# Latent attention in a four-layer model: keys mapped per head, scores over 32 rows in row quarters

## The reference, cut to what matters

```python
c_q = h_t @ W_DQ + b_DQ                     # 32 numbers per token
c_kv = h_t @ W_DKV + b_DKV                  # 32
q_c = c_q @ W_UQ + b_UQ;  k_c = c_kv @ W_UK + b_UK     # 128 per head
q_r = c_q @ W_QR + b_QR;  k_r = h_t @ W_KR + b_KR      # 32 per head; k_r is shared
q = concat([q_c, q_r]);   k = concat([k_c, k_r])
attn = softmax(q @ k.T / sqrt(128 + 32))
o = (attn @ (c_kv @ W_UV + b_UV)) @ W_O + b_O
```

## Time and profile before

| | |
|---|---|
| three runs | 4379.04, 4382.91, 4383.27 us, median 4382.91 |
| the profiled execution | span 4374.4 us from its first to its last instruction; of its time outside the span nothing is recorded; the runs' median is 8.5 us longer |
| busy in the span | PE 3697.7 us, DVE 3018.0, ACT 2493.0, POOL 1280.4 |
| the stage `latent_heads` | from about 1094 to 1800 us |

### The profile page before, as it was taken

One profiled execution on the slowest core, in us unless ns is written; L12 is line 12 of the kernel. 1 busy time (PEld: TensorE's weight loads), 2 busy tenths in 40 slices (PEclk: granted clock), 3 DMA queues, 4 the chain that ended last, 5 costly groups with the idle time before them and its releaser, 6 DMA issues. The chain is left out here.

```text
span 4374.4 us, 86127 instructions
## 1 busy us (share of the span) xinstructions
PE 3697.7 (85%) x32769; PEld 1693.5 (39%) x32773; DVE 3018.0 (69%) x4604; ACT 2493.0 (57%) x5084; POOL 1280.4 (29%) x1223
## 2 busy tenths in 40 slices
PE   5769998753999999787999997878995689999957
PEld 4523333633333333342222223445654512222237
DVE  6567774557656665658999994435994489999933
ACT  3436666463244444533888887434543448888844
POOL 2610000524488887000000000035883500000016
PEclk7879999776999999886999999888997879999979
DMA  3221110210000000002000000050001120000012
GB/s 122 71 77 37 41 42 15 82 34 9 1 4 6 4 4 4 17 1 71 25 28 31 28 24 3 18 130 10 1 1 64 56 78 23 31 31 24 19 54 73
DMA packets 80436, 152.55 MB, mean 35 GB/s; under 512 B 20492, under 2 KB 46748, under 8 KB 79132
## 3 DMA queue, kind: packets, MB, share of 16 engines
q1 hardware_dynamic: 54408, 105.15, 7.4%
q0 software_dynamic: 12704, 22.97, 1.8%
q10 hardware_dynamic: 12916, 18.93, 1.3%
HBM read 103.75 MB, written 31.20 MB: 31 GB/s over the span
## 5 line engine op out<-in xcount | busy, mean ns | idle before, releaser
L1516 DVE TENSOR_REDUCE 32_heads_mx<-32_heads_mps 128x1 f32<-128x1024 f32 x512 | 602.4, 1219 | 48.0 <-PE 32_heads_mps L1366 45.5
L1516 DVE TENSOR_REDUCE 55_heads_mx<-55_heads_mps 128x1 f32<-128x1024 f32 x512 | 602.5, 1219 | 46.4 <-PE 55_heads_mps L1366 43.7
L1486 ACT ACTIVATE 32_heads_p<-32_heads_sps 128x512 f32<-128x512 f32 x1024 | 553.7, 596 | 86.4 <-PE 32_heads_sps L1392 83.2
L1486 ACT ACTIVATE 55_heads_p<-55_heads_sps 128x512 f32<-128x512 f32 x1024 | 553.7, 596 | 85.9 <-PE 55_heads_sps L1392 82.6
L2528 ACT ACTIVATE 21_latent_heads_p<-21_latent_heads_ring 128x512 f32<-128x512 f32 x512 | 277.4, 595 | 360.0 <-PE 21_latent_heads_ring L2447 360.0
L1516 DVE TENSOR_REDUCE 7_heads_mx<-7_heads_mps 128x1 f32<-128x1024 f32 (+7 forms) x384 | 333.6, 908 | 147.6 <-PE 7_heads_mps L1374 101.9
L2551 DVE TENSOR_REDUCE 21_latent_heads_mx<-21_latent_heads_ring 128x1 f32<-128x512 f32 x512 | 322.9, 684 | 146.7 <-PE 21_latent_heads_ring L2426 146.7
L1486 ACT ACTIVATE 7_heads_p<-7_heads_sps 128x512 f32<-128x512 f32 (+3 forms) x640 | 308.1, 533 | 156.0 <-PE 7_heads_sps L1395 116.5
L1392 PE MATMUL 32_heads_sps<-30_head_rows_qs,30_head_rows_ks 123*32 123x512 bf16 x4096 | 314.4, 383 | 8.3 <-ACT 32_heads_p L1486 5.0
L1392 PE MATMUL 55_heads_sps<-51_head_rows_qs,51_head_rows_ks 123*32 123x512 bf16 x4096 | 314.3, 383 | 8.2 <-ACT 55_heads_p L1486 5.0
L2443 PE MATMUL 21_latent_heads_ring<-21_latent_heads_qc,17_mla_mem_keys 64*128 64x512 f32 x1024 | 273.0, 610 | 3.6 <-DMA 18_mla_loop_mem_mrow<-21_latent_heads_mT 3.6
...
## 6 DMA issues: line engine op xcount, KB each, us to landing
...
```

Source lines behind the costliest of these rows:

```text
L1486: act.activation(pslot[x % PS][:, 0:CW - off], sps[e % SB][:, 0:CW - off], ACT.Exp, scale=SCALE / 2).then_inc(ex_done, 1)
L1516: dve.tensor_reduce(mx[h % 2][:, i, half:half + 1], mps[x % 2][:, 0:w], AX.X, ALU.max).then_inc(mx_taken, 1)
```

## The change

- Keys go through the head's matrix, not queries. `make_keys` multiplies `maps` (head's matrix, its 32 columns written four times, so that the result stands in all four quarters of the partitions) with `keys`, gives `kh`, 32 rows in each quarter, and ACT copies it out, 1024 columns at a time. `cq` holds c_q alone, in four quarters, for all heads.
- Score and maxima passes contract over 32 rows. Their two matmuls use row quarters 0 and 1 in one pass and 2 and 3 in the next (`rows`).
- What belonged to the row of ones now depends on the key alone: `tilt`, one number for each key and head. It is computed once before head 0 (16 matmuls into `ops`), split in three bfloat16 parts by DVE, turned by 8 transposes, copied by ACT, and carried by 4 DMAs a head into `k_side`, whose other rows are -1. A bfloat16 pair adds it in every maxima pass (with `ones`), and one pair adds it and takes off the maximum in every score pass (`k_side` with `q_side`). The maximum's rows go into `q_side` by 4 DMAs (2 before).
- A ring buffer is now one tensor of 1024 columns; DVE takes one maximum of 1024 columns (32 a head, 64 of 512 before), ACT one exponential of 1024 (64 of 512 before).
- POOL adds up slots 0 to 23 (22 adds a head, two buffers `psum` by turns), DVE slots 24 to 31 into `dsum` (6 adds a head). For head 7 DVE does all. `denominators` moves from slot 4 to slot 6 and goes over both sums, 8 matmuls for 4.
- The product's copy to `osb` moves from DVE to ACT, after slot 1's exponential (DVE for head 7). The copies into `Lh` go. POOL clears `q_side` at the stage's start.
- In `mla_prep` the heads' matrices come ahead of the values on PE; `L` and its copies give way to `maps` and `tilt`, filled by DVE and ACT.

The core of the diff:

```diff
-    SUMS = 4
-    FIRST, LAST = SUMS + 2, 24
+    SUMS = 6
+    FIRST, LAST = 6, 24
+    BY_DVE = tuple(range(24, S))
-        ring = [st.ps(f"ring{i}", [P, CW]) for i in range(2 * RING)]
+        ring = [st.ps(f"ring{i}", [P, 2 * CW]) for i in range(RING)]
...
+        def rows(number, x):
+            low = DC * (2 * (number % 2) + x)
+            return slice(low, low + DC)
...
                 def max_pair(u, h):
-                    i = u // 2
-                    if u % 8 == 0:
-                        pe.wait_ge(q_copied, NC * h + u // 8 + 1)
+                    i, pair = u % NT, u // NT
+                    if i == 0:
+                        pe.wait_ge(k_copied, 2 * h + pair + 1)
...
                     for x in range(2):
-                        half = slice(KC * x, KC * (x + 1))
-                        pe.matmul(bank(number, x)[:], qc[h % 2][half, tile(i)], keys[half, chunk(2 * (u % 2) + x)],
-                                  start=True, stop=True).then_inc(mx_ready, 1)
+                        r = rows(number, x)
+                        pe.matmul(bank(number, x), cq[r, tile(i)], kh[h % 2][r, chunk(2 * pair + x)], start=True, stop=False,
+                                  tile_position=(r.start, 0))
+                    if u == 0:
+                        pe.wait_ge(tilt_in[h % 2], 64 * (h // 2 + 1))
+                    for x in range(2):
+                        r = rows(number, x)
+                        pe.matmul(bank(number, x), ones[r, :], k_side[h % 2][r, chunk(2 * pair + x)], start=False, stop=True,
+                                  tile_position=(r.start, 0)).then_inc(mx_ready, 1)
...
                 def scores(p, h):
...
                     for x in range(2):
-                        half = slice(KC * x, KC * (x + 1))
-                        pe.matmul(bank(number, x)[:], keys[half, tile(j)], qc[h % 2][half, chunk(2 * (p % 2) + x)],
-                                  start=True, stop=False)
+                        r = rows(number, x)
+                        pe.matmul(bank(number, x), kh[h % 2][r, tile(j)], cq[r, chunk(2 * (p % 2) + x)], start=True, stop=False,
+                                  tile_position=(r.start, 0))
...
+                for t in range(NT):
+                    ins = pe.matmul(ops[:, 8 * t:8 * (t + 1)], keys[0:KC, tile(t)], tilt[0:KC, :], start=True, stop=True)
+                ins.then_inc(tilt_ready, 1)
+                pe.wait_ge(tilt_split, 1)
+                for h in range(MLA_H):
+                    ins = pe.transpose(tilt_rows[0:PARTS, h * P:(h + 1) * P], tilt_parts[:, h].rearrange("p a t -> p (a t)"), g.ident_bf[:])
+                ins.then_inc(tilt_turned, 1)
                 for u in range(U):
                     max_pair(u, 0)
...
-                        for x in range(2):
-                            act.wait_ge(sc_ready, 2 * n + x + 1)
...
+                        act.wait_ge(sc_ready, 2 * n + 2)
...
+                        act.activation(slot(p, h)[:], ring[place["score", h, p] % RING][:], ACT.Exp, scale=MLA_SCALE).then_inc(ex_done, 1)
...
+                        if h and p == 1:
+                            act.wait_ge(pv_done, NT * h)
+                            if h >= 2:
+                                act.wait_ge(o_out, 16 * NC * (h - 1))
+                            act.activation(osb[0][:], ops[:], ACT.Identity).then_inc(o_copied, 1)
...
+                            if p in BY_DVE[2:]:
+                                if p == BY_DVE[2] and h:
+                                    dve.wait_ge(z_done, h)
+                                add(dve, dsum, dve_added, DVE_ADDS * h, by_dve[p % 2], by_dve[p % 2].index(p), h)
```

More of the change, by code:

```diff
@@ new lines, in latent_head_loop, with add @@
+        freed = {place["score", h, p]: (ex_done, S * h + p + 1) for h in range(MLA_H) for p in range(S)}
+        freed.update({place["max", h, u]: (mx_taken, U * h + u + 1) for h in range(MLA_H) for u in range(U)})
+        freed.update({place["keys", h, x]: (k_copied, 2 * h + x + 1) for h in range(MLA_H) for x in range(NC // 2)})
+        assert sorted(freed) == list(range(len(passes)))
+        def add(eng, sums, done, base, order, n, h):
+            x = order[n] % 2
+            eng.wait_ge(ex_done, S * h + order[n] + 1)
+            if n > 1:
+                eng.wait_ge(done[x], base + n - 1)
+            so_far = slot(order[0], h)[:] if n == 1 else sums[:, x, :]
+            eng.tensor_tensor(sums[:, x, :], so_far, slot(order[n], h)[:], ALU.add).then_inc(done[x], 1)
@@ L2461, in denominators @@
                 def denominators(h):
-                    pe.wait_ge(added_even, ADDS * (h + 1))
-                    pe.wait_ge(added_odd, ADDS * (h + 1))
+                    last = h == LASTH
+                    for x in range(2):
+                        if not last:
+                            pe.wait_ge(pool_added[x], POOL_ADDS * (h + 1))
+                        pe.wait_ge(dve_added[x], DVE_ADDS * h + (S // 2 - 1 if last else DVE_ADDS))
                     if h:
```

280 lines of the change are left out of this document (148 added, 132 removed).

## The result

The changed kernel took 4387.65 us (median of 17 runs, 4380.95 to 4400.56), the kernel before 4379.18 (17 runs beside it, 4370.60 to 4384.97): a ratio of 1.0022, 95% interval 1.0014 to 1.0031. The medians differ by 8.5 us (0.19%), about the 9 us that I had set as what a measurement tells from no change, and the interval leaves out 1; I had forecast 16 us faster.

The account below looks back on a forecast made before the run. PE bounds the middle piece now (60.60 of 60.60 us); afterwards the buffer ring sets the pace. Terms -21 (heads 1 to 6) - 8 (head 0) + 1 (head 7) + 12 (front) = -16 us: 4367 us, range 4312 to 4425.

Parts of the forecast that it names:

- The price of a pass: PE, score and maxima passes: 1.07 us with no overlap, 0.54 with full overlap of passes in different row quarters.
- Rival (a): PE: matmuls start strictly in written order, so +3.6 us a head and 4419 us in all; chance 0.17.
- Rival (b): PE: one waiting round per quarter, a pass starts 0.43 us behind its neighbour; +3.2 a head, 4389 us; chance 0.20.
- The ring walk: Middle slots: three buffers set the pace, each turning in 2.65 us, 0.88 a pass; six slots take 15.9 us.
- Six slots take 15.9 ... Nineteen: 50.4: Slots 6 to 24: 50.4 us at the six-slot pace; with 6.8 for slots 6 and 7, 57.1 against 60.6.
- Head 0: First head, without denominators: middle piece 50.4 + 1.9 for keys = 52.3 us, a gain of 8.3.
- A longer wait in front puts a few us there, within that bound: Clock at 0.50 around head 0's start: a few us lost, counted inside the front's +12 (8 to 16).
- Before head 0: Latent heads' front: first maximum +11 us, maxima -0.7, two more DMAs +1.5; together +12 (8 to 16).
- The two key passes and their copies lie beside the tilts: Front, before head 0: key passes and copies run alongside the tilts' 4.8 us, with no time of their own.
- Score-only slots: Slots without maxima: -0.05 us per two slots, +0.6 product copy, -0.9 denominators, +0.3 keys; together nothing.
- Rival (c): Middle: VectorE alone bounds it at 44 us, 16.6 less in each of seven heads; 4280 at the full; chance 0.16.
- the stall: Slots 6 and 7: no maximum read during VectorE's 5.2 us of division; 6.8 us more than two steady slots.

Follow-up runs that it names:

- e1_one_pair: The changed kernel with every pass in row quarters 0 and 1; 1.1422 times the kernel before.
- the two profiles of the change: The changed kernel's first run, 1.0022 times the kernel before, and the same kernel run again without an edit, 1.0007.
- e2_busy_pe: The changed kernel with matmuls nobody reads filling PE's stop before slot 0 of head 0; 1.0004 times the kernel before.
- e3_sums4: The changed kernel with the denominators made at slot 4 and not at slot 6; 0.9955 times the kernel before.
- e12_before_spread: The kernel before with the next head's maxima over slots 4 to 25 and not 6 to 24, denominators still at slot 4; 1.0164 times the kernel before.

## Why the prediction was wrong, step by step

- **The price of a pass** was right: 1.07 us alone (`e1_one_pair`), and passes in free quarters start 0.02 us apart with shared rounds of 0.43, the score-only slots' too (1313.61 and 1313.63). **Rival (a)** falls: a pass's float32 rounds start before the bfloat16 pair that is written ahead of them. The Trainium skill, TensorE: Matmul & The Clock Gate, The mechanism, has starts and ends in program order; in this trace that holds for the first rounds and not for a bfloat16 pair (1261.30) against the rounds of the pass behind it (1260.36). **Rival (b)** falls too. Four row tiles at once take 0.43 us a round, as two do; the 3.07 times one of the Trainium skill, TensorE: Matmul & The Clock Gate, Measured speedup vs the span model, by the prediction's estimate a round of 0.56 us, is not borne out here.
- **The ring walk** was right for the steady slots: fifteen take 39.9 us, 16.0 per six for my 15.9. Slots 6 and 7 took 11.6 for 12.0. **"Six slots take 15.9 ... Nineteen: 50.4" is the term that failed in the heads.** I used the mean of the pattern for seventeen slots (45.1). They took 47.1: fifteen of them go by the pattern, but the two that are left over are both slots with a product (slot 8, with two maxima passes, 3.8 us; slot 24, with one, 3.4), 7.2 us for the 5.3 of two mean slots. So a head gains 1.8 and not 3.5: over six heads 10 us of the forecast. The lower end of my exp of 1024, 0.96, took 0.36 for 512 columns more, which no row shows; the exp measured 1.02, my middle value.
- **The clock in slots 6 and 7** was in no term: 2.5 and 4.2 us over six heads (the two profiles of the change). I had walked PE's wait during the division but not asked what the granted clock does after a stop of PE inside a head.
- **Head 0:** -8.3 forecast; as the kernel is, +0.3 in one profile and -5.5 in the other. **"A longer wait in front puts a few us there, within that bound" is the step that failed**: 3 to 9 us, charged to a bound that the front used up by itself. The wait is hardly longer (8.4 us for 7.7); the clock came back 9 to 24 us after slot 0's start for 5.5 before. With the clock held up head 0 is -8.7 (`e2_busy_pe`), but that this meets my number is luck: slots 6 to 24 give 6.1 of it (54.5 for 60.6, where I had 52.3), and 2.5 lie in slots 0 to 5 (10.2 for 12.7), for which I had nothing and which in the kernel before ran in part at 0.50. No run fills the stop in the kernel before.
- **Before head 0:** +12 (8 to 16) forecast, +14.8 in the stage and +1.1 in the preparation (12.1 us, with the clock still at 0.50 at its end; 11.1 in `e3_sums4` as in the kernel before, with 1.00 there). **"The two key passes and their copies lie beside the tilts"** failed: on PE they stand in front of them, 3.6 us at half clock, 1.8 at full (`e3_sums4`). The split took 3.9 and not 1.2, because of GpSimd's memsets. The tilts (3.7 for 4.8), the transposes (1.05), the copy (1.02) and the DMAs (4.6 for 4.9) were about right; the maxima and the DMAs before slot 0 came out 1.1 us lower.
- **Score-only slots** unchanged and **head 7** +0.2 for +1: right, or nearly.
- **Sum** for the first profile: +15.9 - 8.6 (heads 1 to 6) + 0.3 + 0.2 = +7.8 where I had -16; for the second about +4.4. That this is near the measured +8.5 and +3 us is in part chance: the first profile is of the slowest of the 17 runs (4400.56), and its span is 24.4 us over that of before. Of the rest, 13.9 lie in one stage that the change doesn't touch (local heads: 128.6 us in the profile of before, 129 to 142 in the others), without a system that I can name.
- **Rival (c)** (VectorE alone bounds the middle) falls for this kernel. The largest thing that I missed is what it points at: with the denominators elsewhere and the maxima spread, the changed kernel takes 75.5 us a head for 84.5. How much of that the row quarters give and how much the spread is not shown, since `e12_before_spread` was spoilt; for the steady slots of the change as it was, the 11.5 us of `e1_one_pair` stand. The prediction had found the stall (6.8 us more than two steady slots) and rightly charged it to the change; that it is by far the largest cost of the change in the heads, 3.7 us of it for the place of the denominators alone, it did not say.
